# A convolution over five tiles of rows: four in two column phases, the short one in four, with the up-sampled band ahead of the next group's splits

## The reference

```python
def _L1_conv_ref(x, base_w, base_b, base_scale, wconv_w, wscale):
    cur = x
    for i in range(3):
        co = haar2d(cur)                 # (ll, lh, hl, hh) of half the size, each times 0.5
        cur = co[:, :, 0]
        flat = co.reshape(B, C * 4, h, w)
        flat = dwconv(flat, wconv_w[i]) * wscale[i]       # 5x5, 'SAME', one filter per channel
        level_coeffs.append(flat.reshape(B, C, 4, h, w))
    next_ll = 0
    for i in reversed(range(3)):
        co = level_coeffs[i].at[:, :, 0].add(next_ll)
        next_ll = ihaar2d(co)            # back to twice the size
    base = dwconv(x, base_w) * base_scale + base_b
    return base + next_ll
# layer 0: x = x + attention(_gn(x));  layer 1: x = x + _L1_conv_ref(_gn(x), ...)
```

## Time and profile before

| | |
|---|---|
| median of three runs | 11,053.4 us |
| profiled execution, its own time | 11,061.64 us |
| its span | 11,059.8 us |
| TensorE matmul, weight load | 10,538.7 us (95%), 8,946.0 us (81%) |
| VectorE, ScalarE, GpSimd | 9,242.7 us (84%), 7,168.6 us (65%), 3,679.7 us (33%) |
| granted TensorE clock, mean | 0.992 |
| in 6,000 to 8,000 us: matmul, VectorE, ScalarE, GpSimd | 1,976.80, 1,562.97, 1,115.73, 528.47 us of 2,000 |
| there: DMA engines, GB/s | 0.71 busy, 155 |
| `xb` or `yb` loads of a group | 240, 256, 256, 256 and 208 KB each |
| `out` stores of a group | 208 KB four times, 192 KB once |
| `raw` loads of a channel | 80 KB four times, 320 KB twice, 160 KB four times |

### The profile page before, as it was taken

How to read it: one execution, slowest core, us unless ns; L and a number is a source line. 1 busy time by engine, 2 the same in 40 slices (tenths; PEclk the granted TensorE clock), 3 DMA queues, 4 the chain that set the end, 5 groups by cost and what they waited for, 6 DMA issues and landing times. The chain is left out here.

```text
span 11059.8 us, 205333 instructions
## 1 busy us (share of the span) xinstructions
PE 10538.7 (95%) x66084; PEld 8946.0 (81%) x66084; DVE 9242.7 (84%) x16479; ACT 7168.6 (65%) x11852; POOL 3679.7 (33%) x3715
## 2 busy tenths in 40 slices
PE   4999999999999999999969999999999999999999
PEld 4888888888888888888858888888888888888887
DVE  6989989899998999988867777777777777777777
ACT  4777777777777777778735555555555555555554
POOL 3444444444444444444322222222222222222222
PEclk9999999999999999999979999999999999999999
DMA  5323333232333333322257777677777767767775
GB/s 185 133 92 126 109 109 126 92 130 95 126 114 104 114 103 115 126 81 74 69 124 154 155 156 154 154 152 155 156 157 157 155 153 156 155 153 154 152 156 125
DMA packets 1162861, 1453.43 MB, mean 131 GB/s; under 512 B 215391, under 2 KB 1125023, under 8 KB 1125279
## 3 DMA queue, kind: packets, MB, share of 16 engines
q1 hardware_dynamic: 1161055, 1442.80, 51.6%
q10 hardware_dynamic: 1376, 6.13, 0.1%
HBM read 1040.11 MB, written 408.56 MB: 131 GB/s over the span
## 5 line engine op out<-in xcount | busy, mean ns | idle before, releaser
L1292 PE MATMUL ps_w<-zb,mat 128*128 128x512 f32 x4800 | 1925.6, 401 | 8.6
L1293 PE MATMUL ps_w<-zb,mat 128*128 128x512 f32 x4800 | 1906.4, 397 | 0.0
L1294 PE MATMUL ps_w<-zb,mat 128*128 128x512 f32 x4800 | 1904.9, 397 | 0.0
L634 POOL CAST xn_hi<-xs 96x512 fp32r<-96x512 f32 x1024 | 840.7, 821 | 3112.3 <-PE ps_qkv L659 2261.1
L1438 DVE SCALAR_TENSOR_TENSOR ob<-ps_w,prm,x 64x512 f32<-64x512 f32 x1920 | 1440.5, 750 | 515.6 <-PE ps_w L1344 476.8
L1243 ACT ACTIVATE z<-x,prm 64x384 f32<-64x384 f32 (+1 forms) x3072 | 1814.0, 662 | 58.8 <-DVE x L1369 51.1
L1185 POOL CAST mat<-raw 128x1280 fp32r<-128x1280 f32 (+1 forms) x288 | 464.7, 1631 | 3947.6 <-DMA raw<-vec 2351.3
L657 PE MATMUL ps_qkv<-wqkv_hi,xn_hi 96*128 96x288 f32 x4096 | 1388.9, 339 | 38.2 <-POOL xn_lo L636 19.9
L636 POOL TENSOR_TENSOR xn_lo<-xs,xn_hi 96x512 fp32r<-96x512 f32 x1024 | 1363.4, 1331 | 81.8
L658 PE MATMUL ps_qkv<-wqkv_lo,xn_hi 96*128 96x288 f32 x4096 | 1214.1, 296 | 0.0
L659 PE MATMUL ps_qkv<-wqkv_hi,xn_lo 96*128 96x288 f32 x4096 | 1211.8, 296 | 0.0
(11 more groups left out here) (196 smaller groups left out, 24154.1 us busy)
## 6 DMA issues: line engine op xcount, KB each, us to landing
xst<-in_x SPq DMA_DIRECT2D x96, 2048.0 KB, 13.8
xs<-in_x SPq DMA_DIRECT2D x128, 1536.0 KB, 8.9
y_scratch<-ys SPq DMA_DIRECT2D x128, 1536.0 KB, 9.5
out<-ob SPq DMA_DIRECT2D x768, 208.0 KB
xb<-in_x SPq DMA_DIRECT2D x576, 256.0 KB
yb<-y_scratch SPq DMA_DIRECT2D x576, 256.0 KB
raw<-vec SPq DMA_DIRECT2D x192, 320.0 KB, 4.2
raw<-vec SPq DMA_DIRECT2D x384, 160.0 KB, 3.9
```

The lines of the kernel that those rows point to most:

```text
L1292: mm(out_, w[HI], xx[HI], start=start, stop=False)
L1293: mm(out_, w[HI], xx[LO], start=False, stop=False)
L1294: return mm(out_, w[LO], xx[HI], start=False, stop=stop)
```

## The change

Five things change, all in the third phase but for the layout of `vec1`.

1. **The tiles.** Four tiles of 64 rows start at the top and the bottom of the image (`TILES`), the outer ones without a halo at the image's edge, and give 60, 56, 56 and 60 rows. A fifth (`SPECIAL`) has 32 rows and gives the 24 in the middle. The masks and the zeroing of whole tiles go.
2. **Four phases for the fifth tile.** Its 32 rows times four column phases fill the 128 partitions, with 64 columns for an image (`zs`). Its filter is three matrices (`STAPS`, `mat_s`), so it takes 9 matmuls of 256 columns. The matrices come from eight more loads a channel (`raw_s`) out of `vec1`, which gets two zero taps at either end; GpSimd makes them beside `mat1`. ScalarE makes `zn` (rows by columns) and `zq` (four phases) from it, `finish` takes it out in four instructions of 32x256.
3. **The sum and the up-sampling** read every second element where the two phase layouts meet, and the low band comes out with even and odd columns apart (`ll1`), so `make_in` reads them side by side.
4. **Order.** VectorE finishes tiles 0 and 1 before `make_in`, tile 2 after it, and does `up_levels` and `split_next` before `trailing`. ScalarE copies `s3` in the middle of `norm` and makes the high parts of `next_ll` before `leading`.
5. **Constants.** `down_sb` and `up_sb` are made on VectorE from the identity, not loaded, and the first loads no longer wait for the zeroing.

The core of the diff:

```diff
-NV1 = 4 * TAPS * 2
+NV1 = 4 * (TAPS + 2) * 2
+SROWS = WROWS // 2
+SPHASES = 128 // SROWS
+STAPS = 3
+BLOCKS = W // SPHASES
+SPECIAL = WINDOWS - 1
+TILES = ((0, 0, WROWS - HALO), (WROWS - 2 * HALO, HALO, WROWS - 2 * HALO),
+         (H - 2 * WROWS + 2 * HALO, HALO, WROWS - 2 * HALO), (H - WROWS, HALO, WROWS - HALO),
+         (2 * WROWS - 4 * HALO, HALO, SROWS - 2 * HALO))
+def tile_place(t):
+    return (t % 2) * WROWS, t // 2, SROWS if t == SPECIAL else WROWS
...
             def zero_pads(eng):
-                for t_ in (xb, yb, *zb[0], *zb[1], *in2_p, in3_hl):
-                    eng.memset(t_[:].bitcast(F32), 0.0).then_inc(zeroed, 1)
+                for t_, n, width in padded_tiles:
+                    for at in (slice(0, n), slice(width - n, width)):
+                        eng.memset(t_[:].bitcast(F32)[..., at], 0.0).then_inc(zeroed, 1)
...
                 def load_raw(c):
...
+                    for ia in range(2):
+                        for q in range(SPHASES):
+                            first = q * SROWS + ia
+                            sp.dma_start(raw_s[first:first + SROWS - 1:2, :, :],
+                                         bass.AP(tensor=vec1.tensor, ...,
+                                                 ap=[[2, SROWS // 2], [V1, SPHASES * STAPS], [1, SROWS]])).then_inc(raw_in, 16)
...
-                sp.wait_ge(zeroed, N_ZERO)
                 load_raw(0)
...
                 def norm(m, k, g, first=False, between=None):
...
+                    for b in range(IMGS):
+                        last = nc.scalar.activation(
+                            zn[:, b], x1_s[own(k, g), b], ACT.Identity, ...)
+                    last.then_inc(zn_set, 1)
                     for p in range(2):
-                        ts = slice(p, WINDOWS, 2)
+                        if p == 1 and between is not None:
+                            between()
+                        ts = slice(p, SPECIAL, 2)
...
+                    for q in range(SPHASES):
+                        last = nc.scalar.activation(zq[q * SROWS:(q + 1) * SROWS].rearrange("p b j -> p (b j)"),
+                                                    zn[:].rearrange("p b w -> p (b w)")[:, q::SPHASES], ACT.Copy)
...
                     def conv(t):
                         pe.wait_ge(out_ready, qn * WINDOWS + (LEAD + t + 1 - WINDOWS))
+                        if t == SPECIAL:
+                            for d in range(STAPS):
+                                split(ps_w[t][:, 0:IMGS * BLOCKS], [mat_s[k][h][:, d, :] for h in range(2)],
+                                      [zs[g][h][:, :, d:d + BLOCKS] for h in range(2)], d == 0, False)
+                            return
...
-                            last = mm(ps_ll[:], down_sb[:, t, :], zb[g][h][:, t, :, 2:2 + HALF], start=t + h == 0,
-                                      stop=t + h == WINDOWS)
+                            mm(ps_ll[:], down_sb[:, t, :],
+                               zb[g][h][:, t, :, 2:2 + HALF].rearrange("p b (j v) -> p v b j", v=2), start=t + h == 0, stop=False)
...
+                            if t == SPECIAL:
+                                for v in range(2):
+                                    last = mm(ps_w[t][:, 0:IMGS * BLOCKS], up_sb[:, at[t] + v, :], half[:, v::2], start=False,
+                                              stop=half is next_b and v == 1)
...
                     if before:
-                        finish(qn - 1, mb, kb, gb_, (0,))
+                        finish(qn - 1, mb, kb, gb_, (0, 1))
                     make_in(qn)
                     if before:
-                        finish(qn - 1, mb, kb, gb_, (1,))
+                        finish(qn - 1, mb, kb, gb_, (2,))
                     split_in(qn)
                     if before:
-                        finish(qn - 1, mb, kb, gb_, range(2, WINDOWS))
+                        finish(qn - 1, mb, kb, gb_, (3, 4))
                     if n is None or n + 2 < GROUPS_C:
                         make_x1(*ahead(m, k, g, 2))
+                    up_levels(qn)
+                    split_next(qn)
                     if n is None or n + 1 < GROUPS_C:
                         trailing(qn + 1, ahead(m, k, g, 1)[2])
-                    up_levels(qn)
-                    split_next(qn)
```

More of the change, by code:

```diff
@@ L1010, in wt_attention_kernel @@
             SLOTS = 4
-            x1 = [sb_(f"x1_{s}", [128, PAIRW, IMGS, W]) for s in range(SLOTS)]
+            x1 = [sb_(f"x1_{s}", [128, SPECIAL // 2, IMGS, W]) for s in range(SLOTS)]
+            x1_s = sb_("x1_s", [SLOTS * SROWS, IMGS, W])
             xb = sb_("xb", [128, PAIRW, IMGS, W])
@@ L1091, in _ @@
             def _(sp):
-                for dst, src in ((down_raw, down), (up_raw, up), (inside_sb[:], inside)):
-                    sp.dma_start(dst, src).then_inc(const_in, 16)
                 def load_prm(c, k):
@@ L1436, in finish @@
                                 dve.wait_ge(prm_in[k], mc * 16 + 16)
-                        for q in range(2):
+                        for q in range(SPHASES if t == SPECIAL else 0):
+                            last = v.scalar_tensor_tensor(
+                                out=ob[0:SROWS, t // 2].rearrange("p b w -> p (b w)")[:, q::SPHASES],
+                                in0=ps_w[t][q * SROWS:(q + 1) * SROWS, 0:IMGS * BLOCKS], scalar=prm[k][own(k, g), 1:2],
+                                in1=x1_s[own(k, g)].rearrange("p b w -> p (b w)")[:, q::SPHASES],
+                                op0=ALU.add, op1=ALU.add)
+                        for q in range(0 if t == SPECIAL else 2):
                             last = v.scalar_tensor_tensor(
@@ new lines, in _ @@
+                dve.wait_ge(down_set, 5)
+                for t, (start, skip, n) in enumerate(TILES):
+                    to = slice((start + skip) // 2, (start + skip + n) // 2)
+                    for v_ in range(2 if t == SPECIAL else 1):
+                        first = skip // 2 + v_ * (SROWS // 2)
+                        v.tensor_scalar(down_sb[:, t + v_, to], pair_sums[:, t // SPECIAL, first:first + n // 2], 0.5, None,
+                                        ALU.mult).then_inc(down_set, 1)
@@ L1477, in _ @@
+                dve.wait_ge(down_set, N_SET)
                 dve.wait_ge(zeroed, N_ZERO)
```

187 lines of the change are left out of this document (106 added, 81 removed).

## The result

The changed kernel takes 11,153.3 us (median of four runs, 11,149.3 to 11,156.8) against 11,053.7 us of the kernel before: a ratio of 1.0085, 95% interval 1.0068 to 1.0103. It is 0.85% slower, where 1.6% faster was forecast, and above the forecast's range. The profiled execution has a span of 11,153.4 us. From `prm` issue to `prm` issue in SyncE's queue a channel takes 57.44 us (36 channels from 6,050.59 to 8,118.43) where it took 56.33; 96 times the 1.1 us are the loss. Not every channel is alike: in 6,000 to 10,000 us they take 56.8 to 58.5 us here, and in the kernel before there are two kinds, 50 of about 56.05 and 20 of about 57.1.

A forecast was written before the change was run, and what follows sets the result against it. A loop through VectorE, SyncE's queue and DMA was taken to bound: 8.6+1.3+8.35+5.6+14.1+16.6 = 54.55 us a channel against 56.34. 96 channels give -172, once-only -8, together -180: 10,873 us by the median, range 10,520 to 11,100.

The forecast's parts named there:

- The queue that I believe decides: Third phase, SyncE's queue: eight more issues delay B's inputs, so a VectorE, SyncE, DMA loop sets 54.55 us a channel.
- The small finish pieces: VectorE, small tile: four 32x256 pieces in place of two 64x512, taken at 1.6 us; bounds 0.3 and 0.75 each.
- VectorE beside GpSimd: VectorE's chain in B, `make_x1` to first finished tile, beside GpSimd: 16.6 us, including 1.5 for the first tile.
- Issues: SyncE's queue: eight `raw_s` issues at 0.7 us each, 5.6 us (3.6 to 6.6), after 8.35 for ten `raw` issues.
- Landing: DMA: inputs shrink to 2,304 KB and take 14.1 us from first input issue to landing.
- Strided reads: TensorE's sum and up-sampling at every second element: taken at nothing, upper bound 2.4 us a group.
- the first rival: TensorE stays the bound: 51.0 us a channel, -521 us, about 10,530; chance 0.15.
- The order: VectorE's next-group splits (3 to 4.5 us) between `next_b` and first finished tile: 0.8 us of stall a channel, in B.
- The clock: TensorE's granted clock: no size given; a fall below 1.00 through idle time was named as a term left out.
- the once-only terms: Outside the channel loop: -11 us for no memset wait, up to 4 us for phase one's vectors; together -8.
- the wrong mechanism: Slower rival: stores get among the inputs on the DMA engines, 57.6 us a channel, about 11,165 us; chance 0.18.
- both small errors upward: No-change rival: issues at 0.825 and small finish pieces at 0.75, 56.9 us a channel, +46 us; chance 0.07.

The follow-up runs named there:

- e1: Changed kernel with the next group's inputs issued right behind the stores, ahead of the raw loads: 10,892.6 us, ratio 0.9829 to the kernel before.
- e3: Changed kernel with the eight `raw_s` loads issued for the first channel only (fresh small matrices left out): 10,867.5 us, ratio 0.9805 to the kernel before.
- e4: Kernel before with its four `raw1` loads split into twelve, eight more issues a channel for the same bytes: 11,431.5 us, ratio 1.0320.
- e10: Changed kernel with its four `raw1` loads split into twelve, eight more issues a channel: 11,742.9 us, ratio 1.0638 to the kernel before.
- e8: Changed kernel with the small tile's finish pieces in one piece, not every fourth column (output columns misplaced): 11,069.8 us, ratio 0.9979 to the kernel before.
- e11: Changed kernel with GpSimd building matrices for the first two channels only (fresh ones left out): 10,863.6 us, ratio 0.9842 to the kernel before.
- e2: Changed kernel with TensorE's strided reads in sum and up-sampling made plain (column sorting left out): 11,175.6 us, ratio 1.0084 to the kernel before.
- e12: Changed kernel with inputs first, plain reads and GpSimd building matrices for the first two channels only (incomplete computation): 10,450.0 us, ratio 0.9466 to the kernel before.
- e13: Changed kernel with the old order of ScalarE's and VectorE's splits put back: 11,885.1 us, ratio 1.0737 to the kernel before.
- e6: Changed kernel with the stores after the late inputs held until VectorE has made x1 from them: 11,155.1 us, ratio 1.0054 to the kernel before.
- e5: Changed kernel with inputs ahead of the raw loads and plain TensorE reads (column sorting left out): 10,805.1 us, ratio 0.9739 to the kernel before.
- e7: Kernel before with the inputs issued ahead of the raw loads: 10,980.1 us, ratio 0.9947.

## Why the prediction was wrong

The mechanism that the prediction named as deciding does decide: inputs behind eight more issues, a DMA wait of `make_x1` once a channel, TensorE idle before the band in B. e1, e3 and e4 show it from both sides, and e10 its direction. What failed is the step "The queue that I believe decides": its sum of 54.55 us a channel, against 56.34 before, where the profile after has 57.69 in the channel shown and 57.43 in the mean of 69. A margin of 1.8 us was put on terms that added up to 2.9 us of error, nearly all upward. Around the loop, as VectorE sees it:

| stretch of the loop | forecast | channel shown | mean of 69 |
|---|---|---|---|
| first finished tile (B) to `make_x1` of A | 8.6 + 1.5 = 10.1 | 11.30 | 11.38 |
| to the first `raw` issue | 1.3 | 1.31 | 1.25 |
| to the first input issue | 8.35 + 5.6 = 13.95 | 14.13 | 14.35 |
| to the inputs' landing | 14.1 | 14.74 | 14.24 |
| `make_x1` of B to the first finished tile | 15.77 - 0.7 = 15.1 | 16.21 | 16.21 |
| sum | 54.55 | 57.69 | 57.43 |

- **The small finish pieces**, +1.1, are one of the two largest terms: 2.71 us for four where 1.6 was taken. I chose the row nearest in columns, an operation that reads and writes in one piece; these write and read every fourth column. The bound of 0.75 held it, the value didn't. e8 shows 0.78 of the 1.1 us to be the stride, and 83 us in the total. The rest of the first row is the clock, below.
- **VectorE beside GpSimd** in B, +1.1, is the other. The chain was taken over from the kernel before, with the same overlap, and from one channel of its shorter kind: the mean there is 16.07, so 0.3 of the miss was in the reading. Since `make_x1` now comes late, GpSimd's casts start 1.5 us after it, at 8034.63, and not 4.4: the 32x1024 `x_s` takes 2.16 us there and 1.27 in A. Without GpSimd the stretch takes 10.96 us and the loop is no longer the bound (e11). That the earlier meeting is what makes it longer is argued, not shown: in e2 the casts start 0.3 us ahead of `make_x1` and the stretch takes 15.7.
- **Issues**, +0.4. In the channel shown the eight took 6.17 us (0.77 each) where 5.6 was taken, and the ten others 7.96 where 8.35 was read; the range of 3.6 to 6.6 held the eight. While they are issued (8008 to 8013) the DMA engines are busy at 0.33 and move 48 GB/s: the issue is the limit there, not the runs of 128 bytes. **Landing** was right in the mean, +0.14.
- **Strided reads** were taken at nothing and cost TensorE 2.2 us a group, near the upper bound of 2.4. That the forecast hardly depends on it was nearly right (at most 0.7 us a channel, by the estimate at e2). But it was wrong for the first rival: TensorE's own floor is 54.45 (e3, e11), not 51.0, so 10,530 us was out of reach for this kernel, and only e12 shows what the 51.0 stood for (50.07). The Trainium skill (SBUF — State Buffer, Door 1: The DMA port swizzle) says that four fp32 values is how far one can stride for free. For a moving operand at every second fp32 value these traces disagree, 0.456 against 0.235 us at the full clock, and the measurement decides.
- **The order** was costed as a price, 0.8 us in B, with splits of 3 to 4.5 us. It is what makes the column phases bearable at all: without it 65.1 us a channel (e13). I compared the new order with a TensorE that waits, not with the old order under ScalarE's longer work (16 pieces of 0.604, four `zn` of 0.586 and four `zq` of 0.659, where there were 16 pieces before, eight of 0.720 and eight of 0.605).
- **The clock** was left out, and it lies on the loop, through the sum and `ll` for which VectorE waits. The granted clock is 0.98 in the window after, 1.00 before. After the idle stretch in B the up-sampling takes 1.94 us in the channels in which it is granted 1.00 and 2.8 in those with 0.50, the lower of TensorE's two levels. From the first finished tile to `make_x1` of A it is 11.2 us where VectorE needn't wait for `ll` and up to 12.2 where it must; the mean of 11.38 makes 0.2 us a channel, some 18 us in all (an estimate). It is 0.8 us a channel in e4 and 1.0 in e2.
- **A, nine matmuls, the once-only terms**: A took 27.23 us, not 25.1, by the strided reads; the nine special matmuls took 1.10 us as forecast. 96 x (57.44 - 56.33) = +107, so of the measured +100 about -7 is left for what happens once, where -8 was taken.

The chance of 0.18 for slower was given to the wrong mechanism (e6). The right one was written down as well, as "both small errors upward", but at 0.07 and priced at +46, because only two of the loop's terms were allowed to err.

## What to carry to other kernels

A queue that issues without waiting is still a resource: count every issue that stands ahead of the next thing that someone waits for, and put loads that nobody needs for a whole channel behind those that are needed in the next group. When a change uses up a slack of 3 us and the forecast rests on 1.8 us of margin in a loop of five terms, let all five err the same way before giving the sign a chance of 0.75. And when one engine's chain becomes late, ask which other engine it then runs beside: the price of its instructions changes with the company. Read such a price off many rounds of the loop, not off one, and ask of every new idle stretch of TensorE what the clock will be behind it and who waits for that work.

## What the runs showed of the hardware

- A moving operand read at every second fp32 value: 0.456 us for 512 columns against 0.235, and about 0.23 against 0.12 for 256. With the stride it hardly depends on the clock: 0.455 to 0.461 us in 139 sums of the changed kernel and down to a granted clock of 0.59; read in one piece it went from 0.24 to 0.43 us in e2 (A and B, the two sums shown).
- TensorE's granted clock in the up-sampling of B: 0.50 in all 66 channels of e2 (4.5 to 5.9 us from the matmul before to this one) and all 60 of e10 (6.6 to 9.9 us), 0.50 to 1.00 in the changed kernel (2.0 to 3.7 us).
- VectorE, four 32x256 operations from PSUM with every fourth column written and read: 672 ns; in one piece 478 ns.
- SyncE issues a load of 24 KB in 16x12 runs in 0.77 us, one of 80 KB in 0.80 (four from 8004.22 to 8007.41), and pieces of 32 and 16 KB of the latter in 0.77 as well (e4, twelve in 9.26): from 16 to 80 KB the price is by the issue, not by its size.
- GpSimd's casts and subtractions beside VectorE's work on SBUF cost 3.7 us a channel where nothing else binds (e5 to e12). With the same start the casts took 3.27, 4.48 (kernel before) or 5.29 us (e7), and VectorE's chain from `make_x1` to the end of `next_b` 16.1, 15.1 or 13.7.
